# Fused delta-rule attention, MLP and FFN block: ScalarE scales the input, two GpSimd steps move

## The reference, cut to what matters

```python
h = layernorm(x)                       # outer norm
x = x + block(h)                       # block: a delta-rule attention and an MLP, both with residuals
x = x + ffn(x)                         # silu(x wg^T) * (x wu^T), then wd^T, hidden size 768

def block(h):
    h = h + delta(layernorm(h)*g + b)  # solve with (I + tril(k k^T)), k normalised, then out_w
    return h + relu((layernorm(h)*mn_g + mn_b) @ w1 + b1) @ w2 + b2
```

## Time and profile before

| | |
|---|---|
| runs | 1764.57, 1763.86, 1760.37 us; median 1763.86 |
| the profiled execution | 1764.44 us, span from first to last instruction 1762.7 us |
| granted TensorE clock, mean | 0.982 |
| busy: PE, DVE, ACT, POOL | 1661.6, 1222.9, 823.7, 895.9 us |

### The profile page before, as it was taken

One profiled execution on the slowest core, in us unless ns is written; L12 is line 12 of the kernel. 1 busy time (PEld: TensorE's weight loads), 2 busy tenths in 40 slices (PEclk: granted clock), 3 DMA queues, 4 the chain that ended last, 5 costly groups with the idle time before them and its releaser, 6 DMA issues.

```text
span 1762.7 us, 31724 instructions
## 1 busy us (share of the span) xinstructions
PE 1661.6 (94%) x11298; PEld 1510.1 (86%) x11298; DVE 1222.9 (69%) x2796; ACT 823.7 (47%) x1754; POOL 895.9 (51%) x1212
## 2 busy tenths in 40 slices
PE   5899999579999999999999999999999999999997
PEld 4899999458888888888888888888888888888886
DVE  4677777237777776777777767777777666666664
ACT  3677777224444444444444444444444444444442
POOL 4456776234555554554444555545545554455551
PEclk8999999789999999999999999999999999999999
DMA  4755565411111121111112311111112111121200
GB/s 116 233 183 190 203 204 201 174 43 44 55 55 55 55 91 55 55 55 55 55 56 64 92 55 55 55 55 55 55 55 79 55 55 55 56 62 63 63 13 25
DMA packets 131700, 145.34 MB, mean 82 GB/s; under 512 B 60885, under 2 KB 113368, under 8 KB 131544
## 3 DMA queue, kind: packets, MB, share of 16 engines
q1 hardware_dynamic: 131544, 143.31, 25.4%
HBM read 82.13 MB, written 61.15 MB: 81 GB/s over the span
## 4 chain that ended last, share of the span: by engine, by line
PE 45%; POOL 19%; issue 8%; DVE 7%; ACT 1%; POOLq 0%; DMA 0%; DVEq 0%; ACTq 0%
PE ps L153 22%; PE ps L1007 14%; POOL xh L1468 5%; POOL xa L1457 4%; POOL xa L1462 4%; PE ps L921 4%; PE ps L938 3%; PE ps L1017 3%; DVE bs L1414 2%; POOL xn L1446 2%; POOL sc L1436 2%; DVE a L1409 2%; DVE wt L1230 1%; POOL sc L1439 1%; PE ps L927 1%
## 5 line engine op out<-in xcount | busy, mean ns | idle before, releaser
L1486 POOL TENSOR_TENSOR hl<-hf,hh 128x512 fp32r<-128x512 f32 x128 | 166.9, 1304 | 401.8 <-ACT hh L1134 401.8
L1017 PE MATMUL ps<-wdT,hh 128*128 128x256 f32 x768 | 204.2, 303 | 0.8 <-ACT sg L1129 0.6
L1017 PE MATMUL ps<-wdT,hl 128*128 128x256 f32 x768 | 187.1, 281 | 2.0 <-DVE hl L1277 2.0
L1134 ACT ACTIVATE hh<-hf 128x512 fp32r<-128x512 f32 x192 | 120.8, 629 | 134.1 <-DVE hf L1272 130.9
L1272 DVE TENSOR_TENSOR hf<-ps,sg 128x512 f32<-128x512 f32 x192 | 132.4, 690 | 66.5 <-PE ps L1007 65.1
L1129 ACT ACTIVATE sg<-ps 128x512 f32<-128x512 f32 x192 | 113.9, 593 | 125.9 <-PE ps L1007 125.7
L1138 ACT ACTIVATE z_hi<-ps 128x256 fp32r<-128x256 f32 x128 | 49.4, 386 | 257.6 <-PE ps L938 257.6
L1007 PE MATMUL ps<-xh3T_hi,wgT 128*128 128x512 f32 x384 | 154.6, 403 | 0.7 <-DVE xh3T_lo L1277 0.7
L1007 PE MATMUL ps<-xh3T_hi,wuT 128*128 128x512 f32 x384 | 152.3, 397 | 0.0
L1007 PE MATMUL ps<-xh3T_lo,wgT 128*128 128x512 f32 x384 | 152.1, 396 | 0.0
L1007 PE MATMUL ps<-xh3T_lo,wuT 128*128 128x512 f32 x384 | 151.9, 396 | 0.0
(11 more groups left out here) (216 smaller groups left out, 5655.7 us busy)
## 6 DMA issues: line engine op xcount, KB each, us to landing
gg_scratch<-gg SPq DMA_DIRECT2D x32, 640.0 KB, 3.3
gg<-gg_scratch SPq DMA_DIRECT2D x32, 640.0 KB, 3.9
kx_scratch<-kx SPq DMA_DIRECT2D x32, 522.0 KB, 2.7
kx<-kx_scratch SPq DMA_DIRECT2D x32, 522.0 KB, 3.6
xk<-in_L_attn_x_dram SPq DMA_DIRECT2D x32, 512.0 KB, 4.2
xt<-in_L_attn_x_dram SPq DMA_DIRECT2D x32, 512.0 KB, 4.7
out_dram<-ot SPq DMA_DIRECT2D x32, 512.0 KB, 2.9
low_scratch<-gg SPq DMA_DIRECT2D x128, 16.0 KB, 1.5
```

Of the source, the lines that this page charges most:

```text
L1017: mm = pe.matmul(ps[:, (FG, FU)[j // 2], (j % 2) * C:(j % 2 + 1) * C], part[:, h, blk(j)], wdT[:, h, :], start=(h == 0 and part is hh), st ...
L1134: act.activation(hh[:, h, :], hf[:, h % 2, :], ACT.Copy).then_inc(hh_ev[h], 1)
L1486: pool.tensor_tensor(hl[:, h, :], hf[:, h % 2, :], hh[:, h, :].bitcast(F32), ALU.subtract).then_inc(hl_ev[h], 1)
```

## The change

Three things. ScalarE takes over the scaling of xt to xh, between wt block 3 and the first relu. GpSimd's sum xt + b2 moves from before the scaling to behind the third norm and the column copy, and waits there for `xh3_done`; the making of xhm_lo gets a wait for the second `h1_lo`. On ScalarE the rounding of z block 3 moves between the two relus of the second half.

```diff
 act_body:
+                        wait(act, xin, i * 16)
+                        for k in range(CB):
+                            after(act, ht_ps[k], i)
+                        after(act, xhm_lo, i)
+                        for j in range(TB):
+                            op = act.activation(xh[:, j, :], xt[:, j, :], ACT.Identity,
+                                                scale=kx[:, E_S + j:E_S + j + 1], bias=kx[:, E_B + j:E_B + j + 1])
+                        op.then_inc(xhm_done, 1)
-                        for m in range(CB):
-                            act.wait_ge(m1_ps[m], i)
-                            act.activation(h12[0][:, m, :], ps[:, (FU, S0)[m], :], ACT.Relu, bias=b1f[:, m:m + 1]).then_inc(h1_hi[m], 1)
-                            act.activation(h1[:, m, :], ps[:, (FU, S0)[m], :], ACT.Relu, bias=b1f[:, m:m + 1]).then_inc(h1_ev[m], 1)
+                    if mlp:
+                        act_relu(act, i, 0, h12[0], h1_hi)
+                        act_relu(act, i, 0, h1, h1_ev)
+                        act_relu(act, i, 1, h12[0], h1_hi)
                     if att:
                         act_z(act, i, 3)
+                    if mlp:
+                        act_relu(act, i, 1, h1, h1_ev)
 pool_body:
-                        pool.wait_ge(kx_in, (i + 1) * 16)
-                        after(pool, xa_done, i)
-                        pool.tensor_tensor(xa[:, :, :], xt[:, :, :], b2_bc[:, :].unsqueeze(1).broadcast_to([P, TB, C]),
-                                           ALU.add).then_inc(xb_done, 1)
-                        for j in range(TB):
-                            op = pool.tensor_scalar(xh[:, j, :], xt[:, j, :], kx[:, E_S + j:E_S + j + 1],
-                                                    kx[:, E_B + j:E_B + j + 1], ALU.mult, ALU.add)
-                        op.then_inc(xhm_done, 1)
+                        if mlp:
+                            pool.wait_ge(h1_lo[1], i)
                         pool.wait_ge(xhm_hi, i + 1)
                         pool.tensor_tensor(xhm2[1][:, :, :], xh[:, :, :], xhm2[0][:, :, :].bitcast(F32),
                                            ALU.subtract).then_inc(xhm_lo, 1)
...
                         pool.tensor_tensor(shf[:, :], kx[:, E_SH:E_SH + TB], zero4[:, :], ALU.add).then_inc(sh_done, 1)
+                        wait(pool, xin, i * 16)
+                        after(pool, xa_done, i)
+                        if mlp:
+                            pool.wait_ge(xh3_done, i)
+                        pool.tensor_tensor(xa[:, :, :], xt[:, :, :], b2_bc[:, :].unsqueeze(1).broadcast_to([P, TB, C]),
+                                           ALU.add).then_inc(xb_done, 1)
```

More of the change, by code:

```diff
@@ L1144, in act_hi, with act_relu @@
                         act.activation(dst[:, k, :], ps[:, banks[k], :], ACT.Copy).then_inc(done[k], 1)
+                def act_relu(act, i, m, dst, done):
+                    act.wait_ge(m1_ps[m], i)
+                    act.activation(dst[:, m, :], ps[:, (FU, S0)[m], :], ACT.Relu, bias=b1f[:, m:m + 1]).then_inc(done[m], 1)
                 def act_body(act, i, att, mlp, down, m, r):
@@ L1168, in act_body @@
                                        bias=zero4[:, 0:1]).then_inc(w_ev[3], 1)
+                        wait(act, xin, i * 16)
[6 more added lines that the diff above has]
+                        op.then_inc(xhm_done, 1)
                     if mlp:
-                        for m in range(CB):
-                            act.wait_ge(m1_ps[m], i)
-                            act.activation(h12[0][:, m, :], ps[:, (FU, S0)[m], :], ACT.Relu, bias=b1f[:, m:m + 1]).then_inc(h1_hi[m], 1)
-                            act.activation(h1[:, m, :], ps[:, (FU, S0)[m], :], ACT.Relu, bias=b1f[:, m:m + 1]).then_inc(h1_ev[m], 1)
+                        act_relu(act, i, 0, h12[0], h1_hi)
+                        act_relu(act, i, 0, h1, h1_ev)
+                        act_relu(act, i, 1, h12[0], h1_hi)
                     if att:
                         act_z(act, i, 3)
+                    if mlp:
+                        act_relu(act, i, 1, h1, h1_ev)
+                    if att:
                         act_z(act, i, 2)
@@ L1458, in pool_body @@
                     if att:
-                        wait(pool, xin, i * 16)
-                        pool.wait_ge(kx_in, (i + 1) * 16)
-                        after(pool, xa_done, i)
-                        pool.tensor_tensor(xa[:, :, :], xt[:, :, :], b2_bc[:, :].unsqueeze(1).broadcast_to([P, TB, C]),
-                                           ALU.add).then_inc(xb_done, 1)
-                        for k in range(CB):
-                            after(pool, ht_ps[k], i)
-                        after(pool, xhm_lo, i)
-                        for j in range(TB):
-                            op = pool.tensor_scalar(xh[:, j, :], xt[:, j, :], kx[:, E_S + j:E_S + j + 1],
-                                                    kx[:, E_B + j:E_B + j + 1], ALU.mult, ALU.add)
-                        op.then_inc(xhm_done, 1)
+                        if mlp:
+                            pool.wait_ge(h1_lo[1], i)
                         pool.wait_ge(xhm_hi, i + 1)
@@ L1478, in pool_body @@
                             after(pool, x2_ev[j], i)
+                        pool.wait_ge(kx_in, (i + 1) * 16)
                         pool.tensor_tensor(shf[:, :], kx[:, E_SH:E_SH + TB], zero4[:, :], ALU.add).then_inc(sh_done, 1)
+                        wait(pool, xin, i * 16)
[4 more added lines that the diff above has]
+                                           ALU.add).then_inc(xb_done, 1)
                     if r == 0:
```

## The result

The changed kernel takes 1722.06 us (median of 4 runs, 1721.1 to 1727.06) against 1764.09 for the kernel before: the ratio is 0.9772, 95% interval 0.9749 to 0.9795. The forecast was 1727, range 1721 to 1742. In a later batch the same two gave 1721.63 and 1761.69, ratio 0.9774 (0.9753 to 0.9794).

The account below looks back on a forecast made before the run. TensorE is nearly full, but GpSimd's chain decides part of each iteration through two TensorE stalls. Terms 12.3, 23.1, 1.6 and 0.6 sum to 37.6 us off 1764.4, forecast as 1727 us, range 1721 to 1742.

Parts of the forecast that it names:

- (a): ScalarE, between wt3 and the first relu: four scalings take 2.09 us, 0.8 us of cover left, no cost on the path.
- (b): GpSimd without scalings and early sum: VectorE's first h_lo no longer stretched to 1.94 us, rounding directly behind the second.
- (c): z_hi between the second two relus starts 0.57 us earlier; TensorE's 0.41 us stall before the z block 2 product closes.
- (d): VectorE's rounding starts at 912.69 instead of 914.01; TensorE's 0.73 us stall on wt before the next z step closes.
- (e): Low half of xhm ends at 915.9 instead of 917.17; TensorE wants it some 1.2 us earlier, so nothing changes.
- (f): GpSimd's sum behind xh3_done ends 0.1 us clear of VectorE's inversion step; moved memset even, within 1 us each way.
- Rival B: The next wait, at TensorE's transposes of x3, takes all the time won: 1764 us; chance 0.05.
- rival A: One of TensorE's two stalls stays: 1741 if the z path stays late, 1750 if only the z path closes; chance 0.13.

Follow-up runs that it names:

- sum_early: The changed kernel with GpSimd's sum of xt and b2 left at its early place, beside VectorE's first h_lo; 1724.11 us, ratio 0.9779 to the kernel before.
- z_only: The kernel before with only z block 3's rounding moved between the two relus, scaling and sum staying on GpSimd; 1758.96 against 1762.32 us, ratio 0.9988.
- z_old: The changed kernel without its z order: z block 3's rounding stays behind both relus; 1737.3 us, ratio 0.9856 to the kernel before.
- scale_pool: The changed kernel with the scaling left on GpSimd, directly behind xa2; 1723.44 us, ratio 0.9775 to the kernel before.
- scale_x2: The changed kernel with ScalarE's four scalings done twice; 1726.19 us, ratio 0.9782 to the kernel before.
- scale_x3: The changed kernel with ScalarE's four scalings done three times; 1811.19 us, ratio 1.0265 to the kernel before.
- sum_nowait: The changed kernel without the moved sum's wait for xh3_done; 1773.62 against 1763.41 us for the kernel before, ratio 1.0063.

## Why the prediction was right, and where its sum was not

The mechanism held: the scalings on ScalarE in their cover, (a); h_lo undisturbed and the rounding directly behind the second, (b); z_hi 0.57 earlier and both stalls closed, (c) and (d); the low half of xhm earlier with nothing waiting for it, (e); the sum clear of the inversion steps, (f). Two of its spare times were not there. In (c) the second h_lo was to be in time by 0.1 us, but it was compared with the start of the seventh multiplication, and the wait stands ahead of the load of its weights, one place earlier in the stream: hence the hole of 0.06. In (f) the 0.1 us were 0.01, which is luck. Rival B did not come: from the z step of block 0 to the transposes of x3 are 0.65 us in both kernels.

*The size.* From the start of the loop's first iteration to that of its last, 31 intervals, the profiled execution went from 1328.65 to 1290.26 us: 38.4 less. The sum of 37.6 was for 30 full iterations and the second one; these intervals hold only 29 full ones, for which its terms give 29 x 1.235 + 0.6 = 36.4. So it was 2 us short. A full iteration gained 1.34, of which I can place 1.33: 0.41 and 0.77 as taken, 0.11 for the z step in full where I counted half, 0.10 for the start behind z_lo that I had not counted (the next multiplication came 0.22 behind it, now 0.12), less 0.06 for the hole at 893.78. The two iterations that start an inversion gained 1.06 and 1.12, so the moved memset, taken as even, cost 0.2 to 0.3 us each: the normalisations are back at 0.73, but the first inversion step waits 1.16 us for GpSimd (at 698.82 in the trace after).

*The other 4 us are from ahead of the loop.* The span of the profiled execution fell by 42.3. The loop starts at 339.5 us instead of 343.8, and the code before it is the same. Whole stretches of 100 us, the first of each kernel, before and after (the columns are the busy time of each engine, then TensorE's granted clock, DMA share and GB/s):

```profile
0.00:100.00 100.00, 74.45 (x470) 68.43 (x471) 55.56 (x160) 51.93 (x149) 44.62 (x125) 0.91 0.56 176
```

```profile
0.00:100.00 100.00, 75.70 (x500) 69.17 (x501) 57.65 (x164) 56.28 (x162) 48.34 (x132) 0.95 0.57 178
```

The granted clock was 0.91 in one and 0.95 in the other. In the traces of the other kernels, with the same code there, the clock is 0.93 to 0.95 and the loop starts between 338.5 and 342.1, so this part scatters by itself. The one trace of the kernel before lies outside both ranges, so it is not shown that scatter is all of it. The first two iterations scatter too: together they take 83.8 us in this trace and 90.9 in that of sum_early. The medians scatter with them (1721.1 to 1727.06 in single runs of one kernel): the variants whose iterations are also 41.56 or 41.57 apart are between 37.2 and 40.2 us faster than the kernel before in their batches, the changed kernel 42.0 and 40.1. So of the 5 us by which the forecast, 1727, lies above the median, some 2 are the sum's, and the rest is of the size of this scatter.

*What failed is the split of the sum.* It priced (c) at 0.41 and (b) with (d) at 0.77, as if each came back alone, and rival A gave 1750 for the z path alone. z_only shows 1759: alone, (c) brings 0.1 us per iteration, for most of what the first stall loses comes back ahead of the seventh multiplication and in the second stall. z_old shows 0.90 for (b) and (d) without it. The two terms add up only once GpSimd's chain is out of the way. And of the two moves in (b) one was not needed: sum_early and scale_pool show that one of the two moves is enough. The prediction even had the number for it: the rounding needed to start 1.3 us earlier, and 3.1 and 2.4 us were taken away. (A slip on the way: the low end, 1764.4 - 37.6 - 5, is 1721.8 and not 1721.5. The measured 1722.06 lies just inside either.)

*The cover of (a) was larger than 0.8 + 1.0 = 1.8.* scale_x2 adds 2.1 us of scaling and costs nothing. The relus, once late, follow each other with no wait for TensorE (894.71, 895.28), and of the 0.2 to 0.3 us that I took for down block 2 only 0.13 came, most of it made up by a quicker start behind it.

## What to carry to other kernels

When one chain of another engine ends behind two stalls of the bottleneck, the stalls are not two terms: find what the last one hangs on, and see by how much that chain must shrink before something else decides; to shrink it further brought nothing here. A step that stands idle for 0.8 us before a wait may have more cover than that (2.1 us of extra work cost nothing here), because the instructions behind the wait can close up. And a GpSimd instruction that moves must be held against VectorE's SBUF-only instructions at its new place, for its full length: the same sum cost nothing in one place, and 1.6 us an iteration in another.

## What the hardware showed

*Beside GpSimd's sum, VectorE stands until the sum ends; it is not slowed by a share:* h_lo took 1.94 to 1.98 us instead of 0.69 beside a sum of 2.39, two normalisations 2.78 instead of 0.73 beside one of 2.52. Beside the four separate scalings of 128x256 on GpSimd an h_lo took only 1.02 (scale_pool), 0.91 (z_only) or 0.70 (the kernel before). VectorE's readers of PSUM beside the moved sum kept their times (0.68, 0.42, 1.29). The Trainium skill, page "VectorE: DVE Perf Modes", section "Why PSUM operands drop a tier", says that the two-port mode needs both SBUF ports and PSUM has one: the trace agrees in that such readers were not held.

*A hole of 2.2 us in TensorE's work cost more than itself in 12 of 29 full iterations.* In scale_x3 the stall is the same in both iterations shown (2.47 us between two starts), yet the 3.5 us behind it went at full clock in one and mostly at the lower level in the next. Two stretches of equal length behind two such stalls (columns as above; the granted clock is the third figure from the end):

```profile
925.50:929.00 3.50, 3.43 (x28) 3.43 (x29) 2.80 (x5) 1.44 (x4) 0.59 (x1) 1.00 0.01 2
969.20:972.70 3.50, 3.46 (x17) 3.46 (x18) 2.56 (x5) 1.41 (x3) 0.62 (x1) 0.56 0.01 1
```

17 multiplications instead of 28 were started in them. At the lower level, 1.2 GHz, 256-column multiplications stood 0.21 us apart instead of 0.12, and the iteration took 45.18 instead of 43.68. Holes of 0.53 and 0.85 us between starts, in the kernel before, did not do this: the clock stood at 1.00 in each 100 us from 900 to 1700. In sum_nowait the usual hole is 1.7 us between starts and was never followed by the lower level; of its two holes of 2.6, in the iterations that start an inversion, one was not (708.26 to 710.84) and one was (1054.18 to 1056.74, then 0.21 us from one multiplication to the next). What decides between two equal holes, no run shows.
